# State-space skip term on TensorE, triangle on GpSimd, expert weights split piece by piece

## The reference

```
# second layer, per sequence of 256 tokens, 4 heads of 64, chunks of 128
z, xBC, dt = split(x @ W_in)
xBC = silu(conv4(xBC));  xh, B, C = split(xBC)
dt = softplus(dt + dt_bias);  A_cum = cumsum(dt * A)
Lmat = exp(A_cum[l] - A_cum[s]) for s <= l, else 0
Y = (C @ B^T * Lmat) @ (xh * dt) + (the state carried over chunks) + xh * D
Y = Y * silu(z);  Y = Y * rsqrt(mean(Y*Y) + eps) * norm_w
x = x + (Y @ W_out) @ W_lin + b_lin
# fourth layer: two of eight experts a token
h = silu(x @ w1[e]^T) * (x @ w3[e]^T);  y = h @ w2[e]^T
```

## Time and profile before

| what | us |
|---|---|
| median of 3 timed runs (lowest, highest) | 1223.52 (1223.49, 1224.08) |
| the profiled execution | 1222.53 |
| its span | 1220.7 |
| busy over the span: PE, DVE, ACT, POOL | 1028.3, 842.0, 712.4, 388.8 |
| mean granted TensorE clock over the span | 0.901 |
| POOL line 851, root, mean of 16 | 1.124 |

### The profile page before, as it was taken

How to read it: one execution, slowest core, us unless ns; L and a number is a source line. 1 busy time by engine, 2 the same in 40 slices (tenths; PEclk the granted TensorE clock), 3 DMA queues, 4 the chain that set the end, 5 groups by cost and what they waited for, 6 DMA issues and landing times. The chain is left out here.

```text
span 1220.7 us, 23165 instructions
## 1 busy us (share of the span) xinstructions
PE 1028.3 (84%) x6680; PEld 898.8 (74%) x6680; DVE 842.0 (69%) x2130; ACT 712.4 (58%) x1561; POOL 388.8 (32%) x421
## 2 busy tenths in 40 slices
PE   2999999999995857999998875567429999899997
PEld 2988988889884624666666664466419999799997
DVE  4577777877766468999999945799845555345554
ACT  4556565565662468889888825666315555355554
POOL 4223232232330000111111112556743444434445
PEclk9999999999998877888888777788559999899999
DMA  5121211211200023232223206534244444333331
GB/s 160 50 82 44 79 50 43 86 43 49 71 0 23 20 69 66 58 69 69 51 54 69 36 1 214 142 126 136 93 136 134 139 128 123 98 90 96 96 97 54
DMA packets 82344, 99.05 MB, mean 81 GB/s; under 512 B 9307, under 2 KB 68194, under 8 KB 82122
## 3 DMA queue, kind: packets, MB, share of 16 engines
q1 hardware_dynamic: 72058, 74.24, 22.5%
q0 software_dynamic: 8752, 21.25, 5.0%
q10 hardware_dynamic: 1440, 2.40, 0.6%
HBM read 72.23 MB, written 27.02 MB: 81 GB/s over the span
## 5 line engine op out<-in xcount | busy, mean ns | idle before, releaser
L1591 PE MATMUL e_p_y<-w,e_gT 128*128 (+1 forms) x852 | 118.2, 275 | 0.0
L1538 DVE TENSOR_TENSOR e_g<-e_sl,e_p_h 128x342 f32<-128x342 f32 x142 | 72.6, 511 | 64.2 <-ACT e_sl L1516 57.2
L1520 ACT ACTIVATE e_gT<-e_p_gx 128x384 f32<-128x384 f32 x142 | 69.8, 491 | 63.9 <-PE e_p_gx L1581 63.9
L1591 PEld LDWEIGHTS e_p_y<-w,e_gT 128*128 128x128 f32 (+1 forms) x852 | 106.1, 191 | 0.4 <-issue 0.4
L87 PE MATMUL e_p_h<-w_hi,e_xT_hi 128*128 x284 | 104.6, 368 | 1.8 <-issue 0.9
L1516 ACT ACTIVATE e_sl<-e_p_h 128x342 f32<-128x342 f32 x142 | 65.0, 458 | 69.9 <-PE e_p_h L89 69.9
L851 POOL TENSOR_TENSOR m_rs<-m_ms,m_minus_half 128x4 f32<-128x4 f32 x16 | 18.0, 1124 | 272.7 <-ACT m_ms L884 272.7
L1542 DVE TENSOR_TENSOR e_xT_lo<-e_p_gx,e_xT_hi 128x128 fp32r<-128x128 f32 x142 | 41.5, 292 | 86.0 <-ACT e_xT_hi L1524 85.6
L1502 POOL DMA_INDIRECT sorted_scratch<-e_xg x71 | 69.0, 972 | 90.7 <-DVE e_xg L1548 87.7
L1500 POOL DMA_INDIRECT out<-e_xg x71 | 68.8, 970 | 87.1 <-DVE e_xg L1548 79.7
L942 DVE SCALAR_TENSOR_TENSOR m_c<-m_p_x,m_vecs,m_c 128x506 f32<-128x506 f32 (+2 forms) x144 | 95.6, 740 | 0.0
(11 more groups left out here) (349 smaller groups left out, 3286.9 us busy)
## 6 DMA issues: line engine op xcount, KB each, us to landing
e_xg<-sorted_scratch SPq DMA_DIRECT2D x142, 130.0 KB, 2.1
m_cum<-cum_scratch SPq DMA_DIRECT2D x16, 1024.0 KB
g_adjT<-in_adjT SPq DMA_DIRECT2D x16, 512.0 KB, 3.8
g_adj<-in_adj SPq DMA_DIRECT2D x16, 512.0 KB, 4.7
c_adjT<-in_adjT SPq DMA_DIRECT2D x16, 512.0 KB, 6.4
x_tokens<-in_x SPq DMA_DIRECT2D x16, 256.0 KB, 4.9
sorted_scratch<-nothing SPq DMA_DIRECT2D x2, 1040.0 KB
sorted_scratch<-nothing SPq DMA_DIRECT2D x12, 130.0 KB, 1.9
```

The lines of the kernel that those rows point to most:

```text
L1520: act.activation(gT[:, c % D3], p_gx[i % 2][:, 0:len(CH)], ACT.Copy).then_inc(q["gT_ready"], 1)
L1538: dve.tensor_tensor(g[:, i % D3], sl[:, i % 2], p_h3[i % 2][:, 0:HP], ALU.mult).then_inc(q["g_ready"], 1)
L1591: last = pe.matmul(p_y[d % 2][:, 0:P], gT[0:r, d % D3, k], w2k[:, bass.ts(e, P)], start=k == 0, stop=k == len(CH) - 1)
```

## The change

Three things change.

1. The skip term xh * D is no longer added by VectorE. A matrix `skip` (the unit matrix times D, made once) is multiplied with xs on TensorE, as the first of now three matmuls a head into `p_zY`, and y1 with its tile is gone: VectorE multiplies `p_zY` with silu(z) at once. Waits that were on y1 are now on y2 or on Y.
2. The triangle is added by GpSimd. Its loop now goes by iteration: triangle of step s (after the transfer of its sums), bias of step s, root of step o.
3. In the routing, GpSimd's line 1197 takes one expert (341 elements) at a time, eight instructions a weight.

```diff
         @block.gpsimd
@@ state-space stage
-            for s in range(STEPS):
-                for half in range(2):
-                    (bias)
-                need(pool, q["x_updated"], T * (s - 1))
-                pool.wait_ge(q["ms_ready"], s + 1)
-                pool.tensor_tensor(rs[:, s % 2], ms[:, s % 2], minus_half[:], ALU.pow)
+            for i in range(END):
+                s, o = i, i - OUT
+                if live(s):
+                    pool.wait_ge(cum_in[s % 2], 16 * (s // 2 + 1))
+                    rows = cum[:, s % 2].rearrange("p h (g b l) -> p h g b l", g=G, b=2)
+                    for b in range(2):
+                        out = rows[:, :, :, b] if b == 0 else late[:, s % 2]
+                        pool.tensor_tensor(out, rows[:, :, :, b], never[:]..., ALU.add).then_inc(q["masked"], 1)
+                    for half in range(2):
+                        (bias)
+                if live(o):
+                    need(pool, q["x_updated"], T * (o - 1))
+                    pool.wait_ge(q["ms_ready"], o + 1)
+                    pool.tensor_tensor(rs[:, o % 2], ms[:, o % 2], minus_half[:], ALU.pow)
         @block.scalar
-                    need(act, q["y1_ready"], 2 * (d - 2))
+                    need(act, q["Y_done"], d - 2)
         @block.vector
+            for k in range(2):
+                dve.tensor_scalar(skip[:, k], eye[:], D[:, k:k + 1], None, ALU.mult).then_inc(q["skip_ready"], 1)
...
-                    dve.wait_ge(q["xs_ready"], y + 1)
-                    need(dve, q["y2_ready"], y)
-                    for k in range(2):
-                        dve.scalar_tensor_tensor(out=y1[:, k], in0=xs[:, y % 3, k], scalar=D[:, k:k + 1], in1=p_zY[:, k], op0=ALU.mult, op1=ALU.add)
-                    dve.wait_ge(q["y1_ready"], 2 * (y + 1))
-                    dve.tensor_tensor(y2[:, y % 2], y1[:], zs[:, y % 3], ALU.mult)
+                    dve.tensor_tensor(y2[:, y % 2], p_zY[:], zs[:, y % 3], ALU.mult)
...
-                if live(s):
-                    (wait for cum_in and the two additions of never)
         @block.tensor
-                    need(pe, q["y1_ready"], 2 * (s - 2))
+                    need(pe, q["y2_ready"], s - 2)
...
+                    pe.wait_ge(q["xs_ready"], v + 1)
+                    pe.wait_ge(q["skip_ready"], 2)
...
-                            pe.matmul(p_zY[p0:p0 + HD, k, l0:l0 + N], xdt[:, v % 2, 2 * g, hs], W[:, v % 2, g, h, 0:N], start=True, stop=False)
+                            pe.matmul(p_zY[p0:p0 + HD, k, l0:l0 + N], skip[:, k, p0:p0 + HD], xs[:, v % 3, k, l0:l0 + N], start=True, stop=False)
+                            pe.matmul(p_zY[p0:p0 + HD, k, l0:l0 + N], xdt[:, v % 2, 2 * g, hs], W[:, v % 2, g, h, 0:N], start=False, stop=False)
@@ routing stage, gpsimd
-                    pool.tensor_tensor(dst.lo[:, :, 0:H], raw[n], dst.hi[:, :, 0:H].bitcast(F32), ALU.subtract).then_inc(q["w_split"], 1)
+                    for e in range(EX):
+                        pool.tensor_tensor(dst.lo[:, e, 0:H], raw[n][:, e], dst.hi[:, e, 0:H].bitcast(F32), ALU.subtract).then_inc(q["w_split"], 1)
```

More of the change, by code:

```diff
@@ L811, in mamba_phase @@
         W = sb("W", [P, 2, G, HEADS, NB])
-        y1 = sb("y1", [P, 2, S])
+        skip = sb("skip", [P, 2, P])
         y2 = sb("y2", [P, 2, 2, S])
@@ L822, in mamba_phase @@
         names = ("consts w2_done w2_ready x_done first_tap taps z_done zs_ready xs_ready B_ready C_ready xh_done xdt_ready G_done "
-                 "masked dec_ready W_ready Y_done y1_ready y2_ready sq_ready ss_done ms_ready rs_ready out_done biased x_updated")
+                 "masked dec_ready W_ready Y_done y2_ready sq_ready ss_done ms_ready rs_ready out_done biased x_updated skip_ready")
         q = {s: sem(s) for s in names.split()}
@@ L844, in _ @@
             bb = b_lin[:].rearrange("p (a d) -> p a d", a=1).broadcast_to([P, 2, P])
-            for s in range(STEPS):
-                for half in range(2):
-                    xt = X[:, s * T + 2 * half:s * T + 2 * half + 2, :]
-                    pool.tensor_tensor(xt, xt, bb, ALU.add).then_inc(q["biased"], 1)
-                need(pool, q["x_updated"], T * (s - 1))
-                pool.wait_ge(q["ms_ready"], s + 1)
-                pool.tensor_tensor(rs[:, s % 2], ms[:, s % 2], minus_half[:], ALU.pow).then_inc(q["rs_ready"], 1)
+            for i in range(END):
[5 more added lines that the diff above has]
+                        out = rows[:, :, :, b] if b == 0 else late[:, s % 2]
+                        pool.tensor_tensor(out, rows[:, :, :, b], never[:].rearrange("p (a b l) -> p a b l", a=1, b=1).broadcast_to([P, HEADS, G, P]), ALU.add).then_inc(q["masked"], 1)
+                    for half in range(2):
+                        xt = X[:, s * T + 2 * half:s * T + 2 * half + 2, :]
+                        pool.tensor_tensor(xt, xt, bb, ALU.add).then_inc(q["biased"], 1)
+                if live(o):
+                    need(pool, q["x_updated"], T * (o - 1))
+                    pool.wait_ge(q["ms_ready"], o + 1)
+                    pool.tensor_tensor(rs[:, o % 2], ms[:, o % 2], minus_half[:], ALU.pow).then_inc(q["rs_ready"], 1)
         @block.scalar
@@ L904, in _ @@
                     dve.wait_ge(q["Y_done"], y + 1)
-                    dve.wait_ge(q["xs_ready"], y + 1)
-                    need(dve, q["y2_ready"], y)
-                    for k in range(2):
-                        dve.scalar_tensor_tensor(out=y1[:, k], in0=xs[:, y % 3, k], scalar=D[:, k:k + 1], in1=p_zY[:, k], op0=ALU.mult, op1=ALU.add).then_inc(q["y1_ready"], 1)
-                    dve.wait_ge(q["y1_ready"], 2 * (y + 1))
                     dve.wait_ge(q["zs_ready"], y + 1)
@@ L912, in _ @@
                     need(dve, q["sq_ready"], y - 1)
-                    dve.tensor_tensor(y2[:, y % 2], y1[:], zs[:, y % 3], ALU.mult).then_inc(q["y2_ready"], 1)
+                    dve.tensor_tensor(y2[:, y % 2], p_zY[:], zs[:, y % 3], ALU.mult).then_inc(q["y2_ready"], 1)
                 if live(v):
@@ L979, in _ @@
                     pe.wait_ge(q["zs_ready"], min(s + 1, STEPS))
-                    need(pe, q["y1_ready"], 2 * min(s - 2, STEPS))
+                    need(pe, q["y2_ready"], min(s - 2, STEPS))
                     pe.wait_ge(q["sq_ready"], o + 1)
@@ L1003, in _ @@
                     pe.wait_ge(q["zs_ready"], min(s + 1, STEPS))
-                    need(pe, q["y1_ready"], 2 * (v - 0))
+                    need(pe, q["y2_ready"], v)
                     if live(o):
@@ L1206, in _ @@
                                                 bounds_check=ROWS - 1, oob_is_err=False).then_inc(q["scattered"], 16)
-            pool.wait_ge(q["w_split"], 2)
+            pool.wait_ge(q["w_split"], 2 * EX)
             pool.wait_ge(q["scattered"], 16 * NT)
```

## The result

The changed kernel takes 1240.24 us (median; 1239.11 to 1240.93), the kernel before 1223.51 us beside it: ratio 1.0138 (95%: 1.012 to 1.0155), so 1.4% slower. Its profiled execution is one of 1240.82 us with a span of 1239.0.

What follows compares the result with a forecast made beforehand. VectorE was taken as full, but TensorE and ScalarE too, with TensorE ending one step in two. State-space stage +16.0 and routing +2.0 on 1222.53 us gave 1240.5 us (1235 to 1247, chance 0.47); 1225 to 1248 held about 0.8.

Steps and rivals of the forecast that it cites:

- what bounds the step: State-space stage: VectorE, TensorE and ScalarE are all full; TensorE sets the end of one step in two, by 1.2 us.
- The round of ScalarE: State-space stage: ScalarE's line 884 comes back after 16.8 us, the lower bound of a step against 17.03.
- part 2: Triangle on GpSimd: 2.45 us a step off VectorE, 4.7 on GpSimd, hidden; no steady step gains, only the start.
- The start: First steps of the state-space stage: taps no longer wait behind the triangle, -6.5 us by 488.80.
- part 1: Skip term on TensorE: +1.73 us a step at the upper clock, 11 steps +19.0; upper bound 3.41 a step.
- The end: Last step with x +1.7; in the drain two Y +6.0 and three y1 gone from the chain, -4.2 us.
- part 3: Routing, weights split by expert: VectorE stays out till the last piece, +1.0 us twice, +2.0.
- rival 1: Routing: VectorE let in between pieces, waiting for one at most; 7.0 us come back, 1231.5 us; chance 0.27.
- Rival 2: State-space stage: longer Y keeps the clock up and ScalarE sets the step; 1213.5 us, chance 0.08.
- Rival 3: Y: skip term paid at the lower clock, or its heads don't run side by side; 1260.5 us, chance 0.10.
- rival 4: Steady steps: half of the skip term vanishes in the slack of the 16.2 us steps; 1230 us, chance 0.08.
- The total: Whole kernel: 1222.53 us for the profiled execution + 16.0 for the state-space stage + 2.0 for the routing = 1240.5.

Runs made afterwards that it cites:

- tri_only: The kernel before with only the triangle moved to GpSimd (skip term on VectorE, weights whole): 1214.6 us, ratio 0.9924.
- skip_gap: The changed kernel with the skip term's matmuls moved from Y to between transposes and wait for xdt, as two wide ones: 1204.2 us, ratio 0.9847.
- tri_fill: tri_only plus two 128x512 matmuls that compute nothing, between the transposes and the wait for xdt: 1207.3 us, ratio 0.9857.
- after_fill: The changed kernel plus two 128x512 matmuls that compute nothing, between the transposes and the wait for xdt: 1212.0 us, ratio 0.9879.
- split_only: The kernel before with only the routing weights split expert by expert: 1222.3 us, ratio 0.9991.
- tri_fill_half: tri_fill with one of its two matmuls that compute nothing: 1213.5 us, ratio 0.9888.

## Why the prediction was right, step by step

**Held: what bounds the step.** That TensorE and not VectorE sets the end of a step is what tri_only shows: VectorE 2.45 us a step freer, the step the same. The round of ScalarE, 16.8 us, named as the floor, is where skip_gap and tri_fill stop.

**Held: part 2.** A triangle instruction on GpSimd takes 2.35 us (2.34 from the earlier trace rows), the root ended before VectorE left the taps (570.6 against 576.4 in the step from 560), and VectorE's wait for xdt is 4.4 us a step, said to be 4 to 6. The first taps end at 436.98, forecast 436.0. The start was forecast at -6.5 us by the fifth x and is -8.1 there (-9.5 in tri_only); by the sixth x it is -3.8, and -6.5 in tri_only. The direction held, and the size was 1.6 us too small.

```profile
569.26 1.23 DVE L930 TENSOR_TENSOR m_xdt<-m_p_hG,table 128x1024 f32<-128x1024 f32 x1 [4.34 <-PE m_p_hG L990]
...
432.30 4.67 DVE L941 SCALAR_TENSOR_TENSOR m_c<-m_p_x,m_vecs,m_c 128x506 f32<-128x506 f32 x7 [0.48 <-ACT m_c L884]
...
569.61 1.03 POOL L859 TENSOR_TENSOR m_rs<-m_ms,m_minus_half 128x4 f32<-128x4 f32 x1
```

**Mis-sized: part 1.** Forecast +1.73 a step, measured +2.28 (25.1 / 11). Even at the upper clock the skip term lengthens Y by 2.16 (5.03 in after_fill, 2.87 in tri_fill). The pitch of a pair of heads is right, 1.08 us against 0.65; what I left out is the end: behind the last pair its odd head's matmuls run alone, 0.43 us more than my four pitches. That the columns go by the upper level held on average, not step by step: in the step from 560.27 Y begins at 573.21 and the clock is 0.50 until 577.5, over half of Y. In the 11 steady steps the low stretch adds 1.54 us to a mean Y before (4.41 - 2.87) and 1.72 after (6.75 - 5.03). So the mean Y grew by 2.34 us, 2.16 of it at the upper clock and 0.18 by more time at the lower one, which covers the 2.28.

**The end, overpaid.** From the last x to the stage's end I forecast +3.5 (+1.7 for the last x step, +6.0 - 4.2 for the drain); it was +0.75. With -1.6 at the start and +6.1 in the steps the errors sum to +1.8: 17.8 for 16.0.

**Wrong: part 3.** Forecast +2.0 with VectorE out till the last piece; the routing is 0.7 us shorter, and 1.45 in split_only. (In the changed kernel's execution the fourth iteration comes 1.5 us later than before, and so it does in tri_fill, which has no pieces.) The forecast wanted line 1294 at over 5 us beside the pieces; the same instruction, now line 1297, takes 0.59. The step that failed took the earlier trace rows as a rule for the pieces. VectorE is let in between pieces, as rival 1 had it and as its sign (under 1 us) says, but rival 1 counted one wait where there are five. Neither counted the dependent instructions. The two chains of five took 5.60 and 4.85 us before and 4.05 and 4.32 after, so of rival 1's 7.0 us some 1.5 came back (split_only). The Trainium skill ("SBUF — State Buffer", "Who interferes with whom") has the exclusion for a whole instruction, with which the 0.82 to 0.84 us beside pieces of 0.87 agree; that the order of issue decides agrees with these too, and not with 3.30 us behind four instructions of which three came later.

**The rivals.** Rival 2 (the clock stays up, 1213.5) did not come to pass: the longer Y stands behind the place where the clock falls, and the clock went on falling (0.86); but its price is near what was measured when the clock was held up (after_fill, 1212.0). Rival 3 (its sum comes to 1260.7, not 1260.5) paid 3.41 a step, rival 4 saw half of it absorbed; the steps show neither. The total came out, 1240.5 against 1240.8 in the profiled execution (median 1240.2), since the stage was 1.8 us too cheap, part 3 was 2.7 too dear, and 1.2 us lie in stages that the change leaves alone. That it agrees within 0.3 us is luck: the steps alone were off by 6.1 us, and start, end and part 3 happened to pay for it. What was earned is the direction and the term behind it, TensorE's longer Y.

## What to carry to other kernels

When work moves to an engine that is full, look for the place in its order where it stands idle, before counting what the work costs: the same columns were +27 us of stage inside Y and made the stage shorter in the gap ahead of a wait. Look there for TensorE's clock above all; a short idle time in every step can cost more than the idle time itself (here 1.3 us idle, and up to 3.3 us by the low stretch), and work that computes nothing, put into it, tells in one run whether it does. A low stretch costs only in the steps whose end TensorE sets. When splitting an instruction that shuts out another engine, count the dependent instructions that will each meet a piece, and see what else queues on the splitting engine where the pieces go.

## What the runs showed of the hardware

- The granted clock fell after sums of squares, transposes and a wait of 1.3 us, in nearly every step, and was 0.50 for 3.4 to 6.8 us. With 1.9 us of matmuls between the transposes and the wait it stayed at 1.00 in most steps (0.97 and 1.00 over 196 us); with half of that it fell in every second step (0.91).
- In the changed kernel, whose steps TensorE ends, a low stretch lengthened a step by half of its own length: 16.74 us without one, 18.4 with 3.4 us, 20.05 with 6.8 us. In tri_only a step with 3.4 us at 0.50 took 16.23 us, and with one matmul of filling and no low stretch (tri_fill_half) 16.16.
- A small VectorE instruction with two inputs in SBUF that began 0.04 to 0.55 us after the start of a GpSimd addition was let in as that one ended, though another addition followed back to back. One that began 0.70 to 1.22 us after the start stayed out through all additions that followed: one more (1.32 to 1.85 us), two (2.31 to 2.70), three (3.11 to 3.30). Where memsets followed in place of additions, one that began 0.87 to 1.00 us after the start was let in as the addition ended (0.29 to 0.42). This is read from the traces of all fourteen kernels, and no kernel was made to test it; what the time since the start stands for is open. It would explain why and the pieces differ.
- A scatter by GpSimd counts too: c_scale began 0.85 us after the start of one and was out until the bias behind it had ended, 1.46 us. The time since the start does not sort these in the same way: c_den began 0.41 us after the start of a scatter with a bias right behind it and was out through both, 1.90 us (857.73 in the kernel before).
